# Graph attention layer on one core: TensorE's relation products move from the group's begin to between the first aggregation and the second addition of sums

## The reference, cut

```python
K, V, Q = ...                               # (nodes, 4 heads, 64)
mod_k  = K[src] + 0.2 * rel[edge_type][:, None, :]
scores = einsum('ehd,ehd->eh', Q[dst], mod_k) / 8
ex     = exp(scores - segment_max(scores, dst)[dst])
w      = ex / segment_sum(ex, dst)[dst]
agg    = segment_sum(w[:, :, None] * V[src], dst)
...
x = x + layernorm(agg @ Wo + bo + xn) * gamma + beta + mixer(xn)
out = x + experts(layernorm(x))
```

## Time and profile before

| | |
|---|---|
| timed runs | 1272.78, 1277.14, 1271.19 us; median 1272.78 us |
| the profiled execution, first to last instruction | 1421.9 us |
| mean granted TensorE clock in it | 0.931 |
| busy: PE, DVE, ACT, POOL | 1131.1 (80%), 926.8 (65%), 833.7 (59%), 799.9 us (56%) |
| the edge stage in it | from about 176 to 997 us |

### The profile page before, as it was taken

The page is one execution under the profiler, slowest core; times in us unless marked ns, Lnnn a source line. Parts: engine busy times, 40 slices in busy tenths (PEclk is TensorE's granted clock), DMA queues, the critical chain, the costliest instruction groups (busy, mean ns, idle before and its releaser), DMA issues. The chain is left out here.

```text
span 1421.9 us, 27109 instructions
## 1 busy us (share of the span) xinstructions
PE 1131.1 (80%) x7282; PEld 862.9 (61%) x7283; DVE 926.8 (65%) x2064; ACT 833.7 (59%) x2962; POOL 799.9 (56%) x835
## 2 busy tenths in 40 slices
PE   5999845888788878888888878886689369999993
PEld 3777623555555555555555556564578257888882
DVE  7676446788788787887787877883787632223231
ACT  3444300677677767777677767776257446666661
POOL 4766665566566665666566655630464135666662
PEclk9999955899999999999999999999899579999997
DMA  7233375677677666776667676740922463343334
GB/s 223 104 116 125 116 219 166 178 197 202 172 199 202 195 194 180 200 199 197 176 194 205 195 202 172 196 130 1 343 103 75 152 189 60 59 64 64 64 60 115
DMA packets 131582, 220.56 MB, mean 155 GB/s; under 512 B 24900, under 2 KB 89580, under 8 KB 131400
## 3 DMA queue, kind: packets, MB, share of 16 engines
q0 software_dynamic: 48832, 138.49, 37.1%
q1 hardware_dynamic: 82632, 80.63, 18.3%
HBM read 188.00 MB, written 34.25 MB: 156 GB/s over the span
## 5 line engine op out<-in xcount | busy, mean ns | idle before, releaser
L611 POOL DMA_INDIRECT KV<-kv,ixs x464 | 473.5, 1020 | 298.9 <-issue 117.7
L627 ACT ACTIVATE KV<-KV,WS 128x65 f32<-128x65 f32 x1792 | 453.3, 337 | 20.7 <-issue 14.7
L719 PE MATMUL ps_o<-KV,PM 128*128 128x260 f32 x928 | 257.0, 400 | 46.6 <-issue 33.6
L725 PE MATMUL ps_o<-ACC,ident 128*128 x464 | 164.7, 438 | 86.8 <-issue 34.7
L700 PE MATMUL ps_qe<-Q,PT 128*128 x1392 | 206.0, 289 | 14.6 <-DVE KV L806 9.5
L719 PEld LDWEIGHTS ps_o<-KV,PM 128*128 128x128 f32 x928 | 161.5, 193 | 89.5 <-issue 66.4
L635 ACT COPY ACC<-ps_o 128x260 f32 x232 | 84.5, 364 | 191.0 <-remote 137.9
L700 PEld LDWEIGHTS ps_qe<-Q,PT 128*128 128x128 bf16 x1392 | 141.8, 102 | 68.3 <-issue 20.3
L806 DVE TENSOR_TENSOR KV<-KV,ps_qe 128x512 f32<-128x512 f32 x232 | 148.7, 668 | 12.2 <-remote 9.4
L725 PEld LDWEIGHTS ps_o<-ACC,ident 128*128 128x128 f32 x464 | 73.1, 194 | 134.3 <-issue 126.4
L799 DVE TENSOR_TENSOR KV<-KV,ps_u 128x1024 f32<-128x1024 f32 x116 | 139.8, 1205 | 11.0 <-remote 11.0
(11 more groups left out here) (297 smaller groups left out, 1686.4 us busy)
## 6 DMA issues: line engine op xcount, KB each, us to landing
dlb<-dl_rows SPq DMA_DIRECT2D x116, 128.0 KB
W<-in_f_W_dram SPq DMA_DIRECT2D x16, 512.0 KB, 6.2
tyb<-ty_rows SPq DMA_DIRECT2D x116, 64.0 KB
KV<-kv,ixs POOLq DMA_INDIRECT x464
kv<-kvb SPq DMA_DIRECT2D x25, 258.0 KB, 2.5
xs_rows<-xs SPq DMA_DIRECT2D x25, 256.0 KB, 2.6
VB<-kv SPq DMA_DIRECT2D x5, 650.0 KB, 8.4
X<-in_x_dram SPq DMA_DIRECT2D x5, 640.0 KB, 10.1
```

The lines of the kernel that those rows point to most:

```text
L611: pool.indirect_dma_start(kv[:, c % KR, n, :], None, d["kv"], bass.IndirectOffsetOnAxis(ap=T["ixs"][:, c % KR, n:n + 1], axis=0)).then_inc ...
L627: m = a.activation(part, part, ACT.Copy, scale=W[:, c % 2, s * H + h:s * H + h + 1])
L719: m = pe.matmul(T["ps_o"][:, p % 2, 0:A], PM[:, p // 2 % 2, p % 2 * 2 + k, :], kv[:, c % KR, 2 * x + k, C:KVW], start=(k == 0), stop=False)
L725: pe.matmul(T["ps_o"][:, p % 2, 0:A], T["ident"][:, :], ACC[:, bass.ds(at, A)], start=False, stop=True).then_inc(s_o, 1)
```

## The change

`relations(G_)` is called after `aggregate(p)` and ahead of `add_sums(p)`. Nothing else changes: no instruction is added or taken away, and no other engine's list is touched.

```diff
                     if G_ < NG:
                         at = rows(G_)
-                        relations(G_)
                     if p >= 1:
                         add_sums(p - 1, before)
                     if G_ < NG:
                         queries(2 * G_, at[0])
                     if p >= 0:
                         to = blocks(p)
                         aggregate(p)
+                    if G_ < NG:
+                        relations(G_)
+                    if p >= 0:
                         add_sums(p, to[0])
                         before = to[1]
                     if G_ < NG:
                         queries(2 * G_ + 1, at[1])
```

## The result

The changed kernel takes 1289.4 us (median), the kernel before 1274.4 us in runs on the same chip. The ratio is 1.0109, 95% interval 1.0089 to 1.0129: 13.9 us slower (0.0109 x 1274.4; the interval is 11.3 to 16.4). One of the changed kernel's four timed runs, 1352.5 us at a granted clock of 0.816, was a slow one: the median counts it, the ratio leaves it out. The forecast was slower by 11.7 us, which lies in that interval.

A forecast was written before the change was run, and what follows sets the result against it. The prediction took VectorE to pace the timed runs, with TensorE's signal prompt or nearly. 1272.8 us plus 0.45 us at 26 chunk boundaries (11.7 us) gave 1284.5, stated as 1284 us; range 1262 to 1294, slower at 0.47.

The forecast's parts named there:

- VectorE paces the timed runs: Edge stage: VectorE's 5.32 us a group sets the timed pace; the profile's 6.36 us loop can't fit.
- late signal: Edge stage, profile: TensorE's signal to ScalarE's copy some 1.6 us late with gathers in flight; prompt, or nearly, when timed.
- 0.82 us from addition to copy: TensorE's addition of sums to ScalarE's copy: 0.82 us once gathers have drained, 2.47 in the profile; gives a 4.71 us loop.
- the tracing itself delays TensorE: Trace records may push back on the sending engine, delaying TensorE in a profiled run alone; no run showed it.
- Earlier by 0.45: add_sums(p-1), queries(2G) and aggregate(p) come 0.45 us earlier: 48 us in the profile's loop, nothing by itself in timed runs.
- The gap of 0.73 us: TensorE's gap ahead of the second addition, which the products would fill, shrinking it to some 0.3.
- "Later", the products themselves: Relation products come 2.24 us later; margin to VectorE's key addition shrinks from 4.2 to some 2.0 us, still covered.
- "Later by 0.45 when PE has waited at aggregate(p)": Work queued behind the products; at g = 3 it delays the chunk-closing chain: 0.45 us at 26 boundaries, 11.7 us.
- The first eight groups: Groups where products move behind queries(2G) alone: taken as nothing, upper bound 5 us.
- No change: Rival: the chunk-closing chain has slack and VectorE hides everything; 1273 us, chance 0.35.
- Faster: Rival: TensorE's signal is late in timed runs too, so the loop gains the 0.45; about 1250 us, chance 0.18.
- The two spans given for the changed kernel: Profile span after the change: 1374 us if the late signal keeps its 1.6 us, about 1422 if lateness hangs on gathers.

The follow-up runs named there:

- clean profile: Kernel before, unchanged, profiled a second time: span 1275.4 us; ratio to the kernel before 0.9988.
- disturbed execution: The first profile of the kernel before, no edit, which the prediction read: span 1421.9 us against timed runs of 1272.8 us (median).
- doubled kernel: Against the kernel before: at g = 3, from round 2 on, relation products moved behind the aggregation and made twice; ratio 1.0358.

## Why the prediction was right, point by point

**VectorE paces the timed runs.** Right: 541.4 us busy of 550. A late signal has no room there, as the prediction worked out, and the clean profile has the 0.82 us from addition to copy that it took from the drained end of the stage. The thought that the tracing itself delays TensorE is not borne out: the second profile of before was traced too, and runs as the timed runs do. The Trainium skill, "NOTIFIC — Programmer's Manual", The programming model, says that the block may push back on an engine; no run here shows it. Why TensorE's signals were held in that one execution stays open.

**"Earlier by 0.45" is worth nothing.** Nearly: the moves at g = 0 to 2 gain 2.9 us, and a steady chunk is 0.18 us shorter with them alone (21.59). The gap of 0.73 us ahead of the second addition, which the products were to fill, was one of the disturbed execution: in the clean profile the addition at 617.30 follows the aggregation without a gap.

**"Later", the products themselves.** The cover held, with one wait of 0.8 us in the change's profile, but it was sized too large. The products end at 604.00 + 0.52 and VectorE's key addition starts at 605.50 (its row is below): a margin of 0.98 us at g = 3, not some 2.0. Moved a little further, behind the turned weights, it was overdrawn by 0.65.

**"Later by 0.45 when PE has waited at aggregate(p)", at 26 boundaries.** Right in place and sign, and in size by what a steady chunk lost, 0.47 us; but that size is a balance of terms that the prediction did not have. The rows of the chain that are not shown above, before:

```profile
613.27 0.56 DVE L785 TENSOR_SCALAR PT<-dlb,iota_p 128x512 bf16<-128x512 bf16 x1
...
615.59 0.67 DVE L817 TENSOR_TENSOR PM<-iota_f,DC 128x512 f32<-128x512 f32 x1
...
619.11 0.21 ACT L652 COPY WS<-ps_s 128x64 f32<-128x64 f32 x1 [0.71 <-PE ps_s L746]
...
619.96 2.03 ACT L627 ACTIVATE KV<-KV,WS 128x65 f32<-128x65 f32 x8 [0.57 <-ACT RR L653]
621.89 0.35 ACT L635 COPY ACC<-ps_o 128x260 f32 x1
```

After, with that key addition:

```profile
599.87 0.56 DVE L787 TENSOR_SCALAR PT<-dlb,iota_p 128x512 bf16<-128x512 bf16 x1
...
602.20 0.67 DVE L819 TENSOR_TENSOR PM<-iota_f,DC 128x512 f32<-128x512 f32 x1
...
605.50 1.22 DVE L801 TENSOR_TENSOR KV<-KV,ps_u 128x1024 f32<-128x1024 f32 x1
...
606.36 0.21 ACT L652 COPY WS<-ps_s 128x64 f32<-128x64 f32 x1 [0.71 <-PE ps_s L746]
...
607.21 2.02 ACT L627 ACTIVATE KV<-KV,WS 128x65 f32<-128x65 f32 x8 [0.57 <-ACT RR L653]
609.14 0.35 ACT L635 COPY ACC<-ps_o 128x260 f32 x1
```

The chain's terms, in us:

| term | predicted | before | after |
|---|---|---|---|
| VectorE's group to placement end | 2.80 | 2.99 | 3.00 |
| to the aggregation | 0 | 0.06 | 0.06 |
| aggregation, to the next on TensorE | 1.05 | 0.98 | 1.07 |
| the products | (0.45) | 0 | 0.45 |
| addition and queries | 1.29 | 1.19 | 1.29 |
| turned weights to the copy | 0.66 | 0.62 | 0.62 |
| to the first weighing | 0.84 | 0.85 | 0.85 |
| eight activations, to the copy of the sums | 2.03 | 1.93 | 1.93 |
| that copy, to the rescale | 0.38 | 0.56 | 0.56 |
| sum | 9.05, then 9.50 | 9.18 | 9.83 |
| the rescale's wait | 0.22, then 0.67 | 0.25 | 0.50 |
| the scan's wait | not named | 0 | 0.30 |

Before: from VectorE's start of the group at 613.27, the rescale at 622.45. After: from 599.87 to 609.70. The chain grew by 0.65, not 0.45: beside the products' own 0.45 the aggregation leads by 0.09 more to what follows it, and the addition and queries take 0.10 more. VectorE waited for 0.55 of it, 0.30 at the scan and 0.25 more at the rescale, and got 0.08 back in a chunk by its own shorter instructions: 0.47, and 25 steady chunks make the 11.8 us of the first section. That this comes so near to the forecast's 0.45 and 11.7 is luck in part, since the longer chain and the shorter instructions cancel. What the prediction missed is the scan: it followed the weights behind the products, and not the turning of the next scores, which stands there too. The 2.1 us ahead of the second rescale are in no term of it, and no run here shows what they come from.

**The first eight groups, taken at 0.** Right, 1.0004.

**The rivals.** "No change" needed slack in the closing chain; there is none, the rescale waits at 28 boundaries already before (0.25 us at 26 of them). That VectorE is the engine to relieve, as the Trainium skill, "Perfetto Trace Analysis", Identifying the Most-Contended Engine, reads it, is true of the busy share; here the time moved through TensorE's list all the same, because that list decides when VectorE is stopped. "Faster" needed the late signal in the timed runs; it isn't there. Its bound was also mis-worked: 23.1 + 18 = 41 us over 116 groups are 0.35 us a group, not 0.2, so it would have come to some 1235 us, not 1251; nothing in the forecast rests on it. The two spans given for the changed kernel (1374 and 1422 us) rested on that signal too and have no meaning without it.

## What to carry to other kernels

Work that an engine does ahead of a wait is free as far as the wait reaches, and is paid in full when it is moved behind the wait: ask of each moved instruction on which side of its engine's next wait it comes to stand, and which chain waits behind that. An engine at 98% still loses time where a chain that runs through the other engines ends on it, so read its waits at the one place of the period where they lie, and take the chain apart there: turning the weights ahead of the aggregation gained as much as the order of the products cost. Where the profiled execution is much longer than the timed ones, take its durations but not its waits.

## What the runs showed of the hardware

One execution in the earlier trace rows had TensorE's signals held back by some 1.6 us with the gathers in flight; two later profiles with a larger DMA share (0.83 and 0.81 against 0.68) had them prompt.

TensorE's granted clock fell to 0.50 (1.2 GHz) at some chunk boundaries with a wait of 1.39 to 1.49 us ahead of the aggregation, and not at others with the same wait: in the doubled kernel at 11 of 26, in the kernel moved at g = 3 only at 2 of 26. In the change itself, with waits of 0.96 to 1.01 in the steady stretch, the granted clock was 1.00 there, and VectorE's scan never waited over 0.6 us. The Trainium skill, "TensorE: Matmul & The Clock Gate", Part 1: The HAM clock gate, says that the array's clock is 1.2 GHz when the engine is idle or cold; the rows have that level, here behind a short wait in a stretch that was busy otherwise (4.00 of 4.00 us from 590 to 594 in the doubled kernel, then the wait of 1.49). Where a wait grows it can so cost twice, once as a wait and once as a slower engine.

GpSimd issued the gathers without a pause in the kernel before: 427.1 us busy and 123.7 between issues from 250 to 800 us, 550.8 of 550. After the change it waited 19.4 us there for TensorE's additions. VectorE waited 0.5 us for gathers in that stretch, so GpSimd didn't hold up VectorE by late gathers, but it is as full as VectorE, and why one-hots and gathers get shorter or longer together with the order on TensorE wasn't tried.
